# Attention and a gated feed-forward over 16 batches: the once-per-batch work in other steps, jobs ahead of the value products, the value bias through spare rows, value blocks evacuated by ScalarE

## What is computed

```
q, k, v = xn Wq + bq, xn Wk + bk, xn Wv + bv        (per head)
att     = softmax(q k^T / 8, causal mask) / 8
attn    = concat over tokens and heads of (att v), reshaped (b, h, s, dh) -> (b, s, h*dh), @ proj
base    = xn W^T
logits  = l2norm(xn Wp^T + bp) @ l2norm(sim) * exp(min(temp, clamp));  lw = softmax(logits)
ret     = lw where it is the largest of the 4 experts, else 0
res     = sum over experts e of ret_e * (xn Wd_e^T) Wu_e^T          (ranks 1, 2, 4, 8)
out     = x + attn + base + res
```

## Time and profile before

| | |
|---|---|
| median of 3 runs (lowest to highest) | 1411.64 us (1411.59 to 1412.21) |
| the profiled execution | 1412.28 us, its span 1410.0 us |
| busy, share of the span: PE, DVE, ACT, POOL | 98%, 81%, 73%, 69% |
| TensorE's granted clock, mean | 0.997 |
| one batch (1 to 14), first scores to first scores | 85.7 to 86.5 us |

### The profile page before, as it was taken

How to read it: one execution, slowest core, us unless ns; L and a number is a source line. 1 busy time by engine, 2 the same in 40 slices (tenths; PEclk the granted TensorE clock), 3 DMA queues, 4 the chain that set the end, 5 groups by cost and what they waited for, 6 DMA issues and landing times. The chain is left out here.

```text
span 1410.0 us, 34925 instructions
## 1 busy us (share of the span) xinstructions
PE 1378.1 (98%) x11036; PEld 1156.6 (82%) x11036; DVE 1141.5 (81%) x4134; ACT 1029.9 (73%) x3032; POOL 966.7 (69%) x1414
## 2 busy tenths in 40 slices
PE   6999999999999999999999999999999999999997
PEld 4778888788888888888888888888878888788886
DVE  6888878878788887977889788787878878888784
ACT  4777777777777776777777777777777777777774
POOL 5767767666676776767667676775776767677663
PEclk9999999999999999999999999999999999999999
DMA  6544444444454445444444544444444444444441
GB/s 154 117 102 103 116 112 94 110 116 102 106 116 115 94 106 123 95 115 100 113 109 109 121 95 106 113 113 106 103 110 112 98 117 110 113 100 112 106 98 46
DMA packets 113010, 151.91 MB, mean 108 GB/s; under 512 B 18175, under 2 KB 47166, under 8 KB 112830
## 3 DMA queue, kind: packets, MB, share of 16 engines
q1 hardware_dynamic: 112830, 149.68, 45.2%
HBM read 11.20 MB, written 4.19 MB: 11 GB/s over the span
## 5 line engine op out<-in xcount | busy, mean ns | idle before, releaser
L534 POOL TENSOR_TENSOR prob<-prob,rden 128x128 f32<-128x128 f32 (+3 forms) x1024 | 710.0, 720 | 383.4 <-DVE rden L796 381.1
L807 DVE CUSTOM_DVE_ANT_0 prob<-scores,mask 128x128 f32<-128x128 f32 (+3 forms) x1024 | 459.0, 484 | 233.1 <-issue 220.0
L611 ACT ACTIVATE prob<-prob,nmax 128x128 f32<-128x128 f32 (+3 forms) x1024 | 565.4, 556 | 69.1 <-DVE nmax L807 67.4
L1058 PE MATMUL ptp<-ident,prob 128*128 128x128 f32 x2560 | 370.5, 274 | 1.7 <-DVE pt L819 1.0
L622 ACT ACTIVATE pt<-ptp 128x128 f32<-128x128 f32 (+3 forms) x512 | 221.1, 432 | 170.3 <-PE ptp L1058 168.1
L1046 PE MATMUL scores<-k_twice,q_parts 128*128 128x128 f32 (+3 forms) x1024 | 328.4, 331 | 9.8 <-DMA k_twice<-k_hi 5.0
L1049 PE MATMUL scores<-k_low,q_parts 128*128 128x128 f32 (+3 forms) x1024 | 320.6, 323 | 0.0
L1058 PEld LDWEIGHTS ptp<-ident,prob 128*128 128x128 f32 x2560 | 295.4, 140 | 29.4 <-POOL prob L534 4.3
L1082 PE MATMUL zp<-pt,v_sb 128*64 128x64 f32 (+3 forms) x4096 | 307.7, 303 | 0.8 <-DVE z_lo L825 0.8
L1082 PEld LDWEIGHTS zp<-pt,v_sb 128*64 128x64 f32 x4096 | 221.5, 137 | 50.4 <-issue 22.3
L1046 PEld LDWEIGHTS scores<-k_twice,q_parts 128*128 128x128 f32 x1024 | 193.4, 189 | 67.8 <-issue 24.0
(11 more groups left out here) (141 smaller groups left out, 1689.7 us busy)
## 6 DMA issues: line engine op xcount, KB each, us to landing
k_twice<-k_hi SPq DMA_DIRECT2D x512, 128.0 KB, 2.4
q_parts<-q_hi SPq DMA_DIRECT2D x256, 128.0 KB, 2.4
q_parts<-q_lo SPq DMA_DIRECT2D x256, 128.0 KB, 2.4
xin<-in_L_attn_x_dram SPq DMA_DIRECT2D x16, 256.0 KB, 3.6
xres<-in_L_attn_x_dram SPq DMA_DIRECT2D x16, 256.0 KB, 3.1
out_dram<-osb SPq DMA_DIRECT2D x16, 256.0 KB, 2.5
pt<-in_L_attn_Wq_dram SPq DMA_DIRECT2D x1, 512.0 KB, 4.4
pt<-in_L_attn_Wk_dram SPq DMA_DIRECT2D x1, 512.0 KB, 4.8
```

The costliest lines, as they stand in the source:

```text
L534: nc.gpsimd.tensor_tensor(part, part, scale, ALU.mult).then_inc(pn_ready, 1)
L611: nc.scalar.activation(part, part, ACT.Exp, bias=nmax[:, s % NROT, h:h + 1], scale=-1.0, accum_out=den[:, s % NROT, h:h + 1]).then_inc(p_r ...
L807: nc.vector.tensor_tensor_reduce(out=prob[:, s % NROT, h, 0:cols], in0=scores[h][:, 0:cols], in1=mask[:, S - cols:S], scale=-INV_SCALE, sc ...
L1058: done = nc.tensor.transpose(ptp[h][:, P * j:P * j + P], prob[:, s % NROT, h, P * j:P * j + P], ident[:])
```

## The change

1. **Order in a TensorE step.** The job now stands right after the transposes, then the transposes of the sum (`STEP_OUT`), then value products and projection, then base and lora. Before, value products and projection came first.
2. **Steps.** router 5 to 1, gated 26 to 17, the last value block 21 to 22; GpSimd's products 8 to 3, its inverse root 12 to 5; VectorE's router chain starts at slot 8 (step 4) for 23 (step 11), with its fifth to seventh slots two later; the experts' exponential 17 to 9; statistics 15, 19 to 5, 9, their sum 20 to 13, variance 21 to 17; the layernorm's three GpSimd operations from step 21 to 18, 19 and 21; sum transposed at 21 for 22, final add 21 for 23; base 23 to 24, lora 29 to 24.
3. **Value blocks.** ScalarE evacuates all eight with the scale alone; VectorE's L717 is gone. The bias comes in through 32 spare rows of the lora matmul: `gated_t` gets 32 constant rows that mark the heads of a row, and `wut` 32 rows that hold bv @ proj of each head, high and low. They are made once, in batch 0 (8 matmuls in step 2, two VectorE operations in step 3, and GpSimd set-up operations).
4. **xt.** ScalarE copies xt first, then xq_hi, then xt_hi; VectorE makes xq_lo first and then xt_lo, both from the SBUF copy `xt` instead of PSUM. The done signal still comes with the second.
5. ScalarE's copy of the sum stands ahead of the exponentials of step 20.

The diff, cut to its core:

```diff
@@ -79,10 +80,10 @@
         JOBS[(NBLK * _p - LEAD[_kind]) % UNITS] = (_kind, _p)
-JOBS[5] = ("router", 0)
+JOBS[1] = ("router", 0)
 JOBS[25] = ("xt", 0)
-JOBS[26] = ("gated", 0)
-V_STEPS = (29, 30, 2, 6, 10, 14, 18, 21)
+JOBS[17] = ("gated", 0)
+V_STEPS = (29, 30, 2, 6, 10, 14, 18, 22)
...
@@ -91,13 +92,14 @@
 HI_KINDS = ("q", "k", "xt")
-STEP_ROUTER, STEP_GATED = 5, 26
-STEP_EVAC, STEP_BASE, STEP_OUT, STEP_FINAL, STEP_LORA = 20, 23, 22, 23, 29
-STEPS_STATS, STEP_AGGR, STEP_VAR = (15, 19), 20, 21
+STEP_ROUTER, STEP_GATED = 1, 17
+STEP_EVAC, STEP_BASE, STEP_OUT, STEP_FINAL, STEP_LORA = 20, 24, 21, 21, 24
+STEPS_STATS, STEP_AGGR, STEP_VAR = (5, 9), 13, 17
+STEP_RSTD, STEP_CENTRE, STEP_SCALE = 18, 19, 21
 STEP_XRES = 28
-STEP_PRODUCTS, STEP_UNORM, STEP_EXPERTS = 8, 12, 17
+STEP_PRODUCTS, STEP_UNORM, STEP_EXPERTS = 3, 5, 9
 R_CHAIN = 14
-R_FIRST = 23
+R_FIRST = 8
...
@@ -387,8 +396,11 @@
             load_weights(2, Wv)
-            sp.dma_start(bv_b, bv.rearrange("h d -> (h d)").partition_broadcast(P)).then_inc(bv_loaded, 16)
             sp.wait_ge(zeroed, 8)
+            for part in range(2):
+                for odd in range(2):
+                    sp.dma_start(bv_rows[GATED + H * part:GATED + H * part + H, DH * odd:DH * odd + DH], bv)\
+                        .then_inc(bv_loaded, 16)
...
@@ -469,10 +481,13 @@
             nc.gpsimd.memset(small_in[:, 1:3, :], 0.0).then_inc(zeroed, 1)
+            nc.gpsimd.memset(bv_rows, 0.0).then_inc(zeroed, 1)
             nc.gpsimd.memset(k_low[:].bitcast(F32), 0.0).then_inc(zeroed, 1)
+            nc.gpsimd.memset(token_heads, 1.0).then_inc(zeroed, 1)
+            nc.gpsimd.memset(late_rows[:], -1.0).then_inc(zeroed, 1)
...
                 nc.gpsimd.memset(ramp[:, :, e:e + 1], float(NEXP - e)).then_inc(zeroed, 1)
-            pool.wait_ge(zeroed, 8 + NEXP)
+            pool.wait_ge(zeroed, 11 + NEXP)
...
@@ -484,13 +499,17 @@
                                         base=odd, pattern=[[-1, P]], channel_multiplier=2).then_inc(consts_ready, 1)
-            def layernorm(c):
+            def root(c):
...
                 nc.gpsimd.tensor_tensor(rstd[:], var_eps[:], power[:, 0, :], ALU.pow).then_inc(rstd_ready, 1)
+            def centre(c):
+                pool.wait_ge(var_ready, c.at(1, 2))
...
                     .then_inc(ln_centred, 1)
+            def scale_rows(c):
...
@@ -498,14 +517,33 @@
             pool.wait_ge(consts_ready, 3)
-            layernorm(Counts(pool, -1))
+            before = Counts(pool, -1)
+            root(before)
+            centre(before)
+            scale_rows(before)
+            def rows_from(tile, step, base):
+                nc.gpsimd.affine_select(out=tile, in_=tile, compare_op=ALU.is_ge, fill=0.0, base=base,
+                                        pattern=[[step, tile.shape[1]]], channel_multiplier=-ROWS * step)\
+                    .then_inc(heads_marked, 1)
+            rows_from(token_heads, 1, ROWS * GATED)
+            pool.wait_ge(heads_marked, 1)
+            rows_from(token_heads, -1, ROWS - 1 - ROWS * GATED)
+            nc.gpsimd.affine_select(out=late_rows[:], in_=late_rows[:], compare_op=ALU.is_ge, fill=0.0,
+                                    base=-(GATED + H), pattern=[[0, 1]], channel_multiplier=1).then_inc(heads_marked, 1)
+            pool.wait_ge(heads_marked, 2)
+            nc.gpsimd.tensor_tensor(gated_t[:], token_heads[:, 0:S], token_heads[:, S:2 * S], ALU.add)\
+                .then_inc(heads_marked, 1)
+            pool.wait_ge(heads_marked, 4)
...
                 scaled = 0 if setup else c.fixed(c.head(s, 1))
-                pool.wait_ge(zeroed, 8 + NEXP)
+                pool.wait_ge(zeroed, 11 + NEXP)
...
@@ -557,8 +595,12 @@
                         pad_low_keys(c, s)
-                    if s == STEP_VAR and not last:
-                        layernorm(c)
+                    if s == STEP_RSTD and not last:
+                        root(c)
+                    if s == STEP_CENTRE and not last:
+                        centre(c)
+                    if s == STEP_SCALE and not last:
+                        scale_rows(c)
...
@@ -578,13 +620,17 @@
                 bank = bank_of(s)
-                if kind not in HI_KINDS:
+                if kind not in HI_KINDS and kind != "v":
...
                 act.wait_ge(job_ready[bank], c.job(s, back))
+                if kind == "v":
+                    nc.scalar.activation(v_sb[:, n % NBLK, S * (n // NBLK):S * (n // NBLK) + S], jobp[bank][:], ACT.Copy,
+                                         scale=INV_SCALE).then_inc(job_done[bank], 1)
+                    return
                 if kind == "xt":
-                    nc.scalar.activation(xt_hi[:], jobp[bank][:], ACT.Copy)
-                    nc.scalar.activation(by_parity(xq_hi[:]), evens_first(jobp[bank][:]), ACT.Copy)
-                    nc.scalar.activation(xt[:], jobp[bank][:], ACT.Copy).then_inc(job_hi[bank], 1)
+                    nc.scalar.activation(xt[:], jobp[bank][:], ACT.Copy).then_inc(xt_ready, 1)
+                    nc.scalar.activation(by_parity(xq_hi[:]), evens_first(jobp[bank][:]), ACT.Copy).then_inc(xq_hi_ready, 1)
+                    nc.scalar.activation(xt_hi[:], jobp[bank][:], ACT.Copy).then_inc(job_hi[bank], 1)
...
@@ -649,10 +695,10 @@
                     evacuate_pt(c, unit)
+                if s == STEP_EVAC and not first:
+                    evacuate_sum(c)
...
                     exponentials(c, s)
-                if s == STEP_EVAC and not first:
-                    evacuate_sum(c)
...
@@ -695,6 +741,13 @@
                 src = jobp[bank]
+                if kind == "v":
+                    return
+                if kind == "xt":
+                    dve.wait_ge(xt_ready, c.at(1, 2))
+                    dve.wait_ge(xq_hi_ready, c.at(1, 2))
+                    nc.vector.tensor_tensor(by_parity(xq_lo[:]), evens_first(xt[:]),
+                                            by_parity(xq_hi[:].bitcast(F32)), ALU.subtract)
...
@@ -709,21 +762,14 @@
                 elif kind == "xt":
-                    nc.vector.tensor_tensor(xt_lo[:], src[:], xt_hi[:].bitcast(F32), ALU.subtract)
-                    done = nc.vector.tensor_tensor(by_parity(xq_lo[:]), evens_first(src[:]),
-                                                   by_parity(xq_hi[:].bitcast(F32)), ALU.subtract)
-                elif kind == "v":
-                    cols = slice(S * (n // NBLK), S * (n // NBLK) + S)
-                    done = nc.vector.scalar_tensor_tensor(
-                        out=v_sb[:, n % NBLK, cols], in0=src[:], scalar=INV_SCALE, in1=bv8[:, cols],
-                        op0=ALU.mult, op1=ALU.add)
+                    done = nc.vector.tensor_tensor(xt_lo[:], xt[:], xt_hi[:].bitcast(F32), ALU.subtract)
...
                 else:
-                    done = nc.vector.tensor_copy(gated_t[:], src[0:PARTS * PART, :])
+                    done = nc.vector.tensor_copy(gated_t[0:GATED, :], src[0:GATED, :])
...
@@ -791,6 +835,15 @@
                 nc.vector.tensor_scalar(simn[:], sim_unit[:], gate_scale[:, 0:1], None, ALU.mult).then_inc(simn_ready, 1)
+            def value_bias():
+                dve.wait_ge(bias_bank_ready, 1)
+                dve.wait_ge(heads_marked, 4)
+                link(nc.vector.tensor_copy(bias_hi[GATED:P, :], outp[GATED:P, 0:E]))
+                link(nc.vector.scalar_tensor_tensor(
+                    out=wut[GATED:P, :], in0=bias_hi[GATED:P, :].bitcast(F32), scalar=late_rows[GATED:P, 0:1],
+                    in1=outp[GATED:P, 0:E], op0=ALU.mult, op1=ALU.add))
...
@@ -847,16 +900,16 @@
                     nc.vector.tensor_reduce(lg[:, 0, :, :], uprod[:], AX_X, ALU.add).then_inc(r_chain, 1)
-                if t == 4:
+                if t == 6:
...
                         .then_inc(r_chain, 1)
-                if t == 5:
+                if t == 7:
...
                     nc.vector.tensor_reduce(row[:, 0, :], logits, AX_X, ALU.max).then_inc(r_chain, 1)
-                if t == 6:
+                if t == 8:
...
@@ -1027,11 +1082,21 @@
                 nc.tensor.transpose(zp[:, P:P + NRD], small_in[0:NRD, 1, :], ident[0:NRD, 0:NRD])
+                pe.wait_ge(bv_loaded, 64)
+                nc.tensor.transpose(zp[:, 3 * P:4 * P], bv_rows, ident[:])
...
                     .then_inc(small_bank_ready, 1)
+            def value_bias():
+                pe.wait_ge(small_ready, 4)
+                pe.wait_ge(proj_loaded, 16)
+                for n in range(NPAIR):
+                    done = nc.tensor.matmul(outp[:, 0:E], bvt[:], projs[:, n, :], start=n == 0, stop=n == NPAIR - 1)
+                done.then_inc(bias_bank_ready, 1)
...
@@ -1125,6 +1190,10 @@
                     transpose(c, unit)
+                if not tail and s in JOBS and not (last and s in AHEAD):
+                    job(c, s)
+                if s == STEP_OUT and not first:
+                    transpose_sum(c, tail)
...
@@ -1134,16 +1203,12 @@
```

(4 more changed lines are left out.)

26 lines of the change are left out of this document (18 added, 8 removed).

## The result

The changed kernel takes **1461.0 us** (median of 4 runs, 1460.5 to 1462.4) against 1411.9 for the kernel before; the ratio is 1.035, 95% interval 1.033 to 1.036. The forecast was 1445 with a range of 1416 to 1462: right in sign and just inside the range, 16 us too low.

The account below looks back on a forecast made before the run. TensorE's stream was taken to bound the kernel, so only its work and waits count. 1412.3 - 13.5 - 3 + 35 + 9 + 3 + 2.5 = 1445.3, less 0.6 gives 1445 us; range 1416 to 1462.

Parts of the forecast that it names:

- order: seams: Seams between kinds of TensorE work, such as 128-wide scores behind the q job: 0.2 us a batch, 3 us in all.
- set-up: Bias matmuls 2 us, the router's early wait for small weights and GpSimd's longer memsets 0.5: 2.5 us lost.
- Part 2: Step 5's transposes wait for VectorE, held in step 4 by GpSimd's products: 2.2 us a batch, 35 us lost.
- Rival A: GpSimd's products are ready in time or their delay holds no transposes: 1410 or 1405 us; chance 0.13.
- Part 3: Step 27's q job, now ahead of the projection, waits 1.6 us instead of 1.04 for VectorE: 9 us lost.
- Rival C: Lighter VectorE has xq_lo and xt_lo earlier, so step 27's q job waits no longer: 1421 us; chance 0.08.
- Part 1: Waits won: 13.5 us in steps 24 and 25 by freed VectorE steps, 3 us in step 0 by ScalarE's value block.
- part 4: Order and set-up: a batch's matmuls stay the same, only seams cost, 3 us; set-up adds 2.5 us.
- Rival B: Each batch's 2.2 us gap drops TensorE's clock to the 1.2 GHz level: 52 us more, 1497 us; chance 0.07.
- granted clock at 1.00 after each gap: Sign expected in the profile after: TensorE keeps its full clock behind every batch's gap of 2.2 us.
- rival D: GpSimd holds up more, by two SBUF inputs and router operations behind long products: 9 us more, 1454; chance 0.12.
- Two SBUF inputs: xq_lo and xt_lo, reading both inputs from SBUF, may wait for GpSimd: taken as 0, up to 9 us.

Follow-up runs that it names:

- values only: Kernel before with only ScalarE's value blocks, the bias by spare rows and xq_lo ahead of xt_lo from the SBUF copy; 1408.4 us.
- both: Changed kernel with VectorE's router reductions at the end of its step 4 and TensorE's job back at the end of its step; 1399.5 us.
- experiment 6: On top of both: the q job of step 27 is released by xq_lo, xt_lo getting a semaphore of its own; 1399.0 us.
- experiments 1, 3, 4 and 5: In this order late reductions, both, old places and values only: old or new places, each with jobs ahead or behind; 1419.0, 1399.5, 1415.4 and 1408.4 us.
- experiment 2: Changed kernel with TensorE's job back at the end of its step, behind value products, projection, base and lora; reductions still early; 1459.6 us.
- after: The changed kernel itself, with the whole change, against the kernel before; 1461.0 us.
- old places: Changed kernel with the once-per-batch work back in the places of the kernel before, jobs still ahead and the value part kept; 1415.4 us.
- late reductions: Changed kernel with VectorE's two router reductions at the end of its step 4, behind the evacuation of head 1's transposes and q_lo; 1419.0 us.
- experiments 9 to 11: First base matmul of step 24 issued four more times in the kernel of experiment 2, four and eight more in after; 1459.4, 1472.7 and 1500.6 us.
- experiment 8: Kernel of experiment 2 with GpSimd's uprod made for one of four experts only, which shortens the gap in step 5; 1424.2 us.
- experiment 9: Kernel of experiment 2 with the first base matmul of step 24 issued four more times, far from the gap; 1459.4 us.

## Why the prediction was right in sign and 16 us low

Its terms, for the whole span, against what was measured:

| term | forecast | measured | from |
|---|---|---|---|
| steps 24, 25 and the other freed places | -13.5 | -15.6 | values only to both: -0.83 a batch, without the 0.21 more in 27 + 28, x 15 |
| step 0 | -3 | -3.5 | 1.79 to 1.56 |
| products' wait | +35 | +33.2 | step 5, 5.70 to 3.56, x 15, and 1.05 in batch 0 |
| q job of step 27 | +9 | +9.6 | 27 + 28, 5.26 to 5.90, x 15 |
| order: seams | +3 | +12.0 | steps 3 and 19, 0.6 x 15; step 17, 0.03 x 16 and 0.25 in ten batches |
| clock | 0 | +8.3 | five stretches of 1.65 |
| set-up | +2.5 | about +5 | what is left, see below |
| sum | +33 | +49 | |

**Part 2 was right in mechanism and size.** Step 8 stood in well for step 4: the forecast had VectorE waiting for 2.2 us and a delay of 2.2 in TensorE's stream, and the rows have 2.06 and 2.14. Rival A (it is covered) falls.

**Part 3 was right in size (0.6 us a batch) and half right in its reason.** "It would be nothing if the job had stayed behind the projection" is wrong: with the job behind, steps 27 + 28 still take 5.48 us for 5.26. TensorE comes there sooner (its step 26 takes 1.57 us for 2.01, without the transposes of `gated`) and VectorE's work from step 26 on has not changed; experiment 6 shows that it is VectorE's sum that counts. Rival C falls with it. That the order of the two subtractions changes nothing holds, even with a release of its own.

**Part 1 was right within 3 us**, 13.5 + 3 forecast and 15.6 + 3.5 measured. It holds only with jobs behind: the square of experiments 1, 3, 4 and 5 shows that the gain of the new places and the loss by the order cannot be had apart.

**The step that failed is part 4**, "the matmuls of a batch are the same", hence order = seams. The working followed one job that the new order put ahead of projection work, the q job of step 27, and not the others that the same edit moved. VectorE evacuates the job of step s-1 at the end of its own step s, however early TensorE made it; TensorE comes to the next job of that bank, in its step s+1, sooner by the products or the projection that now stand behind it (2.3 or 0.7 us). So q of step 3 waits for the router's evacuation in VectorE's step 2, q of step 19 for gated's in step 18, and gated of step 17 for q_lo in step 16. They cost 0.20, 0.40 and 0.28 us a batch (the 0.28 in ten batches, 0.03 in the other six, see below), 12.0 us together for which the sum had 3, and experiment 2 gives them back. The seam that was in the sum does not exist: steps 4, 12, 16 and 20, of width 128 and without a wait, take 1.54 to 1.55 us before and 1.55 to 1.56 after, not 0.05 more.

**Rival B came true in part.** Its all-or-nothing form was wrong, and its chance of 0.07 too low. It was argued away by one stretch at the start, 0.17 us of work in 1.8, which kept the clock; one case could not show that the next keeps it too. The sign "granted clock at 1.00 after each gap" failed in five batches. Gaps of 2.0 us dropped the clock in every third batch, and in batches of other lengths in between 4 and 12 of 15. The Trainium skill ("TensorE: Matmul & The Clock Gate", Why this matters for your kernels) warns of idle gaps over about 3 us only; the runs differ from that rule. The price of a stretch was also off: 1.65 us, not 3.25, since stretches behind a gap of 2 us last 3.41 us and not the start's 6.8.

**That 1461 still lies in the range is partly luck.** The upper end, 1462, was made from rival D's 9 us and the upper bounds of order and set-up. What filled it were the order's 12.0 us, over its own bound of 8, and the clock's 8.3, which the range had left out.

**Two SBUF inputs.** xt_lo takes 0.68 us as ever and xq_lo too, but for two of its sixteen (0.78 us, and 1.26 at the start), which began 0.23 and 0.71 us before the end of a GpSimd instruction, the others at most 0.12; so the 0 was right for them. The effect struck where nobody looked. The conversion of `gated` has moved from step 23 to VectorE's step 15, and by the groups of before and after (busy us, mean ns) it is twice as long:

```profile
L901 DVE CAST gated_parts<-gated 128x256 fp32r<-128x256 f32 x16 | 5.3, 334 | 0.0
```

```profile
L954 DVE CAST gated_parts<-gated 128x256 fp32r<-128x256 f32 x16 | 11.1, 695 | 0.0
```

It now begins within 0.03 us of GpSimd's products, and one of the two gives way. VectorE and GpSimd in batch 1, then in the batch of 821.5:

```profile
156.63 0.28 DVE L954 CAST gated_parts<-gated 128x256 fp32r<-128x256 f32 x1
867.15 0.94 DVE L954 CAST gated_parts<-gated 128x256 fp32r<-128x256 f32 x1
```

```profile
156.60 1.91 POOL L572 TENSOR_TENSOR prob<-prob,rden 128x384 f32<-128x384 f32 x2 [1.61 <-DVE rden L849]
867.12 1.66 POOL L572 TENSOR_TENSOR prob<-prob,rden 128x384 f32<-128x384 f32 x2 [1.61 <-DVE rden L849]
```

Either the conversion takes 0.28 us and the pair of products 1.91, or 0.94 and 1.66. In the ten batches with 0.94 q_lo is late and step 17 takes 4.24 us (4.59 in batch 0), in the other six 3.99: the 0.25 us stand in the table as part of step 17. Rival D (GpSimd holds VectorE up) was right as a mechanism, at 10 x 0.25 = 2.5 us for its 9, and with another instruction. The Trainium skill ("SBUF — State Buffer", Who interferes with whom) names casts among the operations that can take the ports shared with GpSimd, and says that the one to start first blocks the other. The rows agree that one of the two waits the other out; who started first they do not settle, since GpSimd's product is recorded 0.03 us ahead of the conversion in all sixteen batches and is the one that gives way in six.

**Set-up.** The first scores of batch 1 stand at 106.0 us before, 106.4 in values only and 105.9 in old places: the bias matmuls and GpSimd's additions cost next to nothing, not the 2 us of the sum. With the new places it is 108.8 in late reductions, 109.3 in both and 112.6 in after. These are single executions whose starts also differ in clock (6.8 us at the 1.2 GHz level before and in late reductions, 13.7 in values only, both and after), so they tell it only roughly: 2.9 us for the new places, by late reductions, and for after besides the longer start at that level. In after's list of waits:

```profile
PE jobp L1041 <- DVE wut L827: 2.3, 1, 2.3
```

The router of step 1 waits once for the small weights, 2.3 us: that is most of what the new places cost there, and the sum had 0.5 for it together with GpSimd's memsets.

**What is still open.** That the clock's fall goes by where the gap of 2 us lies in time is shown by experiments 9 to 11, and that a shorter gap is safe here by experiment 8. Which places are bad was not worked out, and between 1.3 and 2.0 us no length of the gap was measured. That the late q_lo of step 17 comes from the conversion rests on the rows of the sixteen batches alone; no experiment moved the conversion.

## What to carry to other kernels

Where an edit moves a class of work ("all jobs ahead of the products"), follow every member of it to the buffer that it shares with the one before, not just the one that already waited. A gap of 2 us in TensorE's stream cost more than its length here, and how often depended on where in time it fell, so on the length of everything else in the batch; so the same edit can be worth 20 us without the gap and 1.5 with it, and no edit should be judged in a kernel that has such a gap. A wait for a result that an engine makes in sequence does not go away by waiting for an earlier result, when the next step needs the later ones of the same engine anyway.

## What the runs showed of the hardware

- Idle times of TensorE of 2.0 to 2.1 us, with full work before and after, were followed by 3.41 us at the 1.2 GHz level in 4, 5, 12 or 14 of 15 batches, by the batch's length; 1.3 us never, 3.2 us always, then mostly for 6.83 us. A stretch of 3.41 us cost 1.3 to 1.7 us, one of 6.83 us 2.6 to 2.8.
- In experiment 2 the gap cost the clock in every batch from the second on and the batch settled at one length, 88.7 us. Against it neither after, with 1.1 us a batch more, nor the longer batch of experiment 9, with 0.9 us more, took more than 1.5 us longer in all (1459.6, 1461.0 and 1459.4 us), since both lost the clock in five batches only.
- A VectorE conversion of 128x256 from SBUF to SBUF and a GpSimd product that began 0.03 us earlier took 0.28 and 0.99 us (six batches) or 0.94 and 0.83 us (ten), in one and the same kernel.
